# Three stage starts of a five-stage kernel: normalization ahead of the constants, a semaphore clear behind the first gathers, and an interleaved opening of the last stage

## The reference, cut to what matters

```python
x = x + L0_attn(layernorm(x))   # scan mixer: causal conv, state scan, gate, projection
x = x + L0_ffn(layernorm(x))    # h = layernorm(x); 3-tap conv, 16-head causal attention,
                                # then an expert MLP with one of 4 experts per token
x = x + L1_attn(layernorm(x))   # conv, silu, layernorm, decay exp(delta*A), gate, projection
x = x + L1_ffn(layernorm(x))    # 16 experts: sigmoid scores, best 2 of 4 groups, best 4 experts,
                                # out = sum_e cw_e * relu(x W1_e)^2 W2_e + relu(x Ws1)^2 Ws2
```

## Time and profile before

| | us |
|---|---|
| median of 3 runs | 3261.33 |
| lowest and highest of them | 3254.24, 3273.67 |
| the profiled execution, its own time | 3269.45 |
| its span, first to last instruction | 3267.6 |
| TensorE busy | 2776.8 (85%) |
| VectorE busy | 2128.2 (65%) |
| ScalarE busy | 1628.7 (50%) |
| POOL busy | 1028.5 (31%) |

### The profile page before, as it was taken

How to read it: one execution, slowest core, us unless ns; L and a number is a source line. 1 busy time by engine, 2 the same in 40 slices (tenths; PEclk the granted TensorE clock), 3 DMA queues, 4 the chain that set the end, 5 groups by cost and what they waited for, 6 DMA issues and landing times.

```text
span 3267.6 us, 40411 instructions
## 1 busy us (share of the span) xinstructions
PE 2776.8 (85%) x13719; PEld 1674.1 (51%) x13782; DVE 2128.2 (65%) x3827; ACT 1628.7 (50%) x2433; POOL 1028.5 (31%) x715
## 2 busy tenths in 40 slices
PE   7878887887664789999969999878889887999999
PEld 3445454454452455555536666534344444666666
DVE  0689888889794667777522222146777784777776
ACT  2778777877851345555431111157777781111111
POOL 0888888888861212121010000011121000010000
PEclk9899999999777899999979999978999998999999
DMA  3587888888764765555341000100000002000000
GB/s 109 114 171 152 172 174 169 148 177 175 167 145 90 184 180 92 87 86 88 49 151 49 24 25 23 40 25 7 7 10 11 1 1 59 7 10 11 7 7 13
DMA packets 119272, 262.94 MB, mean 80 GB/s; under 512 B 14784, under 2 KB 72896, under 8 KB 117408
## 3 DMA queue, kind: packets, MB, share of 16 engines
q0 software_dynamic: 24928, 134.89, 19.9%
q1 hardware_dynamic: 94144, 125.47, 16.6%
HBM read 135.40 MB, written 131.20 MB: 82 GB/s over the span
## 4 chain that ended last, share of the span: by engine, by line
PE 52%; ACT 6%; DVE 5%; issue 4%; DMA 1%; POOL 0%; SPq 0%; POOLq 0%; ACTq 0%; DVEq 0%
PE PS L1620 7%; PE PS L2331 7%; PE PS L2349 6%; PE PS L1642 4%; PE PS L1911 4%; PE PS L1284 2%; PE PS L1961 2%; ACT Z L2069 2%; PE PS L1919 2%; PE PS L1263 2%; PE PS L1266 2%; PE PS L1211 2%; PE PS L1241 2%; PE PS L1979 1%; PE PS L1943 1%
## 5 line engine op out<-in xcount | busy, mean ns | idle before, releaser
L804 POOL TENSOR_TENSOR Z<-Z 128x1024 f32<-128x1024 f32 x256 | 647.4, 2749 | 52.8 <-DMA Z<-rows_b 52.7
L714 DVE TENSOR_TENSOR_SCAN Z<-PS,Z 128x1024 f32<-128x1024 f32 x256 | 576.3, 2274 | 17.8 <-POOL Z L804 14.5
L508 PE MATMUL PS<-Z 128*128 128x128 f32 x2048 | 301.3, 293 | 122.0 <-DVE Z L714 49.6
L508 PEld LDWEIGHTS PS<-Z 128*128 128x128 f32 x2048 | 246.8, 150 | 254.6 <-issue 79.9
L646 ACT ACTIVATE PS<-Z 128x511 f32<-128x511 f32 x512 | 332.8, 687 | 68.2 <-DVE Z L714 67.7
L1378 ACT ACTIVATE Z<-PS 128x512 f32<-128x512 f32 x320 | 189.0, 596 | 268.7 <-PE PS L1266 258.0
L2382 ACT ACTIVATE Z<-PS 128x512 f32<-128x512 f32 x144 | 85.9, 596 | 416.8 <-PE PS L2331 416.8
L2331 PE MATMUL PS<-Z 128*128 128x512 f32 x576 | 273.7, 600 | 17.6 <-DVE Z L2464 17.6
L658 ACT ACTIVATE Z<-PS,Z 128x512 f32<-128x512 f32 x378 | 245.5, 683 | 70.0 <-PE PS L508 64.2
L1472 DVE TENSOR_REDUCE Z<-PS 128x1 f32<-128x512 f32 (+2 forms) x384 | 182.6, 507 | 121.7 <-PE PS L1242 118.0
L2069 ACT ACTIVATE Z<-Z 128x2048 f32<-128x2048 f32 x128 | 252.4, 1996 | 12.8 <-PE PS L1961 9.9
(11 more groups left out here) (289 smaller groups left out, 5029.8 us busy)
## 6 DMA issues: line engine op xcount, KB each, us to landing
sums<-Z POOLq DMA_DIRECT2D x112, 768.0 KB, 8.7
Z<-rows_b SPq DMA_DIRECT2D x128, 256.0 KB, 4.8
Z<-scr SPq DMA_DIRECT2D x256, 128.0 KB, 5.2
rows_n<-in_L_ffn_expert_wv POOLq DMA_DIRECT2D x32, 528.0 KB, 8.1
scr<-Z SPq DMA_DIRECT2D x32, 384.0 KB
Z<-Z POOLq DMA_DIRECT2D x14, 768.0 KB, 7.6
Z<-in_L_ffn_expert_wv SPq DMA_DIRECT2D x4, 2048.0 KB, 14.9
Z<-sums SPq DMA_DIRECT2D x7, 768.0 KB, 6.3
```

The source lines that it names most:

```text
L508: ins = e.transpose(self.turned[i % 2][:, c * 128:(c + 1) * 128], self.h(k, c // 2)[:, c % 2, i * 128:(i + 1) * 128], ident)
L714: e.tensor_tensor_scan(h, a, h, 0.0, ALU.mult, ALU.add).then_inc(s["scan"], 1)
L804: e.tensor_tensor(self.h(k, f), self.du[b % 2][:, 2 * f:2 * f + 2, :], b3(self.Bs[k % 2], 1, [128, 2, 512]), ALU.mult).then_inc(s["hin"], 1)
```

## The change

In B, VectorE's constants become a step `consts` at n = -45, behind the second normalization and ahead of the transposes and the taps. Inside it, the wait for POOL's pads is gone (ScalarE's copies, which the taps wait for, keep theirs). TensorE's two waits stand in the first `heads`, ScalarE's in the first `weight`. In D, the clear of stage C's semaphores moves from the end of C into D's `fetch`, behind the four gathers of batch 0. In E, TensorE waits for `d_w` at hidden 0 and VectorE at prep 7, the semaphore of the experts' weights becomes four, each for one group of four experts, and the opening of batch 0 follows the list `START`: five preps, hidden 0, preps 5 to 7, hidden 1, preps 8 to 14, the two downs of the shared expert, hidden 2, preps 15 and 16, hidden 3 and 4, prep 17, hidden 5; from then on come the downs of piece 1 and the order as before. The change has no part in stages A and C; stage A's scan mixer already sums in two chains of accumulating DMAs (even and odd states) in the kernel before.

```diff
--- before.py
+++ after.py
@@ -1037,6 +1037,8 @@
         (33, ("valued", 0), ("values", 1)), (34, ("valued", 1)))
 
     EARLY = -26
+
+    CONSTS = -45
 
     def __init__(self, m):
         self.m = m
@@ -1100,6 +1102,8 @@
         out = []
         for n in range(self.PREP[0][0] - 40, 10 * (N + L + 2)):
             q, u = divmod(n, 10)
+            if n == self.CONSTS:
+                out.append(("consts",))
             if n == self.EARLY:
                 out.append(("load", 0))
             if q % 2 and u == 0 and q > 0:
@@ -1186,9 +1190,6 @@
 
     def pe(self, e):
         m, s, ring, ident = self.m, self.s, self.ring, self.m.ident
-        e.wait_ge(s["d_w"], 80)
-        e.wait_ge(s["ready"], 1)
-
         def bank(*step):
             r = self.uses[step]
             if r >= 2:
@@ -1204,6 +1205,9 @@
                 ins.then_inc(s["prod"], 1)
 
         def heads(b, j4):
+            if b == 0 and j4 == 0:
+                e.wait_ge(s["d_w"], 80)
+                e.wait_ge(s["ready"], 1)
             e.wait_ge(s["hc"], b + 2)
             o = bank("heads", b, j4)
             col = ((j4 // 2) + 2 * (j4 % 2)) * 128
@@ -1370,6 +1374,8 @@
 
         def weight(q, u):
             n = 10 * q + u
+            if n == 0:
+                e.wait_ge(s["ready"], 2)
             e.wait_ge(s["st"], n + 1)
             if n >= 8:
 
@@ -1392,20 +1398,19 @@
                 e.wait_ge(*self.made["route", g // 2 - 1, 6])
             e.activation(self.yf[:, g % 2, :], self.end, ACT.Copy).then_inc(s["end"], 1)
 
-        e.wait_ge(s["ready"], 2)
         self.walk(rstd=rstd, rstd2=rstd2, flipped=flipped, high=high, middle=middle, valued=valued, rowed=rowed, weight=weight,
                   pved=pved, featured=featured, route=self.route.act_steps(e))
 
     def dve(self, e):
         m, s, ring, own = self.m, self.s, self.ring, self.m.own["dve"]
-        e.wait_ge(s["d_w"], 80)
-        e.tensor_copy(m.maskb, self.mask).then_inc(s["ready"], 1)
-        e.wait_ge(s["hc"], 1)
-        self.route.dve(e)
-        e.wait_ge(s["d_sel"], 32)
-        for j in range(2):
-            ins = e.tensor_copy(self.sel[:, 4 * j:4 * j + 4, :].rearrange(FLAT), self.pt[j][0:96])
-        ins.then_inc(s["ready"], 1)
+        def consts():
+            e.wait_ge(s["d_w"], 80)
+            e.tensor_copy(m.maskb, self.mask).then_inc(s["ready"], 1)
+            self.route.dve(e)
+            e.wait_ge(s["d_sel"], 32)
+            for j in range(2):
+                ins = e.tensor_copy(self.sel[:, 4 * j:4 * j + 4, :].rearrange(FLAT), self.pt[j][0:96])
+            ins.then_inc(s["ready"], 1)
 
         def stats(b):
             dve_stats(e, own, lambda i: m.X[:, 4 * b + i, :], self.sb).then_inc(s["moments"], 1)
@@ -1500,7 +1505,7 @@
             rr = m.R2[:, 4 * b + 2 * j:4 * b + 2 * j + 2, :].rearrange(FLAT)
             e.tensor_tensor(rr, rr, self.end, ALU.add).then_inc(s["end"], 1)
 
-        self.walk(stats=stats, norm=norm, stats2=stats2, norm2=norm2, taps=taps, turned=turned, swapped=swapped, most=most,
+        self.walk(consts=consts, stats=stats, norm=norm, stats2=stats2, norm2=norm2, taps=taps, turned=turned, swapped=swapped, most=most,
                   rowed=rowed, backed=backed, projected=projected, route=self.route.dve_steps(e))
 
     def pool(self, e):
@@ -2205,6 +2210,8 @@
                 e.indirect_dma_start(self.gy[i % 4], None, self.c.rows_y,
                                      bass.IndirectOffsetOnAxis(ap=self.c.posy[:, i:i + 1], axis=0)).then_inc(
                                          *self.d_gy.over(i))
+            if b == 0:
+                m.clear(e, 3)
 
         def zx(b):
             e.wait_ge(s["gate"], b + 1)
@@ -2222,6 +2229,9 @@
 
 
     PIECES = 18
+
+    START = (range(5), ("hidden", 0, 0), range(5, 8), ("hidden", 0, 1), range(8, 15), ("down", 0, 0, 0), ("down", 0, 0, 1),
+             ("hidden", 0, 2), range(15, 17), ("hidden", 0, 3), ("hidden", 0, 4), range(17, 18), ("hidden", 0, 5))
 
     def __init__(self, m):
         self.m = m
@@ -2248,16 +2258,19 @@
         self.s = {n: m.sem("e_" + n) for n in (
             "d_w", "moments", "rstd", "nt", "prod", "sig", "ms", "gp", "gmax", "rkd", "rkp", "cw", "up", "relu", "hid",
             "dn", "acc")}
-        self.d_e = m.sem("e_d_e")
+        self.d_e = [m.sem(f"e_d_e{g}") for g in range(4)]
         self.steps = self.order()
 
     def order(self):
-        out = [("prep", 0, p) for p in range(self.PIECES)]
+        out = []
+        for what in self.START:
+            out += [("prep", 0, p) for p in what] if isinstance(what, range) else [what]
         for b in range(NB):
             at = 0
-            out += [("hidden", b, 0), ("hidden", b, 1), ("hidden", b, 2), ("down", b, 0, 0), ("down", b, 0, 1)]
+            if b:
+                out += [("hidden", b, 0), ("hidden", b, 1), ("hidden", b, 2), ("down", b, 0, 0), ("down", b, 0, 1)]
             for x in range(16):
-                if x < 15:
+                if x < 15 and (b or x > 2):
                     out.append(("hidden", b, 3 + x))
                 for i in range(2):
                     out.append(("down", b, 1 + x, i))
@@ -2280,9 +2293,9 @@
         e.dma_start(self.ws2, d["Ws2_t"].rearrange("(k p) m -> p k m", p=128)).then_inc(s["d_w"], 16)
         for g in range(4):
             e.dma_start(self.w1[:, 8 * g:8 * g + 8, :], d["W1_t"][4 * g:4 * g + 4].rearrange(
-                "e (k p) m -> p (e k) m", p=128)).then_inc(self.d_e, 16)
+                "e (k p) m -> p (e k) m", p=128)).then_inc(self.d_e[g], 16)
             e.dma_start(self.w2[:, 4 * g:4 * g + 4, :], d["W2_t"][4 * g:4 * g + 4].rearrange(
-                "e p m -> p e m")).then_inc(self.d_e, 16)
+                "e p m -> p e m")).then_inc(self.d_e[g], 16)
         for b in range(NB):
             e.wait_ge(s["acc"], 34 * (b + 1))
             e.dma_start(m.out.rearrange("b (i p) c -> b p i c", p=128)[b],
@@ -2291,7 +2304,6 @@
 
     def pe(self, e):
         m, s, ring, ident = self.m, self.s, self.ring, self.m.ident
-        e.wait_ge(s["d_w"], 64)
 
         def prep(b, p):
             nf = self.nf[b % 2]
@@ -2324,8 +2336,10 @@
                 e.wait_ge(*ring.done(3 * b + 1))
             if n >= 2:
                 e.wait_ge(s["hid"], n - 1)
-            if j == 2 and b == 0:
-                e.wait_ge(self.d_e, 128)
+            if b == 0 and j == 0:
+                e.wait_ge(s["d_w"], 64)
+            if b == 0 and j >= 2 and j % 4 == 2:
+                e.wait_ge(self.d_e[j // 4], 32)
             for k in range(2):
                 w = self.ws1[:, k, 128 * j:128 * j + 128] if j < 2 else self.w1[:, 2 * (j - 2) + k, :]
                 ins = e.matmul(self.up[n % 2], w, self.nf[b % 2][:, k, :], start=k == 0, stop=k == 1)
@@ -2544,7 +2558,7 @@
                 for n, g in enumerate(stages):
                     g.pool(e)
                     m.stage_end(e, n + 1)
-                    if n < 3:
+                    if n < 2:
                         m.clear(e, n + 1)
```

## The result

The kernel after takes 3250.57 us (median of 20 runs, 3239.05 to 3256.39), the kernel before, run beside it on the same chip, 3264.28 (20 runs). The ratio is 0.9958, 95% interval 0.9945 to 0.9970: a gain of 13.7 us, 9.8 to 18.0. Predicted were 27.1 us and 3234.2, in 3224 to 3249; the result lies outside the range, and as a gain of 0.42% it belongs to what the prediction called within 0.5%.

What follows compares the result with a forecast made beforehand. It took one uncovered chain, held by constants or a semaphore clear, to bound the starts of B, D and E; 10.6 + 2.7 + 13.8 = 27.1 us off 3261.3 gave 3234.2, range 3224 to 3249.

Steps and rivals of the forecast that it cites:

- third rival: Starts of B and E: something other than constants releases the chains; 13 to 16 us at most remain, 3248; chance 0.07.
- Stage B, 10.6: Start of B: statistics start with the stage, the taps begin right behind the sel casts, 10.6 us sooner.
- Stage D, 2.7: Start of D: memset and gathers issue 2.7 us sooner and land 2.7 us sooner; range down to 0.
- Stage E, 13.8: Start of E: hidden 6 starts at 37.0 us instead of 50.8, gain 13.8, bounds 12.0 and 16.2.
- (a): Start of E: the statistics no longer wait for constants, saving 5.9 us; TensorE is free for hidden 0 at 6.6.
- (b): TensorE's order in E's start: hidden 0 3.8 us at low clock, logits 1.8 and hidden 1 1.72 at full clock.
- (c): Start of E: VectorE becomes the chain, `cw` is there at 28.4 us and hidden 6 starts at 37.0.
- The bound for low-clock logits: Start of E: logits at the low clock cost 1.8 us more, giving 12.0 as the lower bound of the gain.
- Stops for instructions: Starts of B and E: one or two instruction-loading stops cut the gain to 21.3 or 15.4, 3240 to 3246; chance 0.11.
- Rival 2: Stage E: threading gains nothing because VectorE's queue delays TensorE; only 5.9 remains there, 19.2 in all, 3242; chance 0.11.
- Rival 4: Stage E: the clock stays at its lower level through batch 0, kernel 38 us longer, 3299; chance 0.03.
- three signs: Idle time called issue in a start, hidden 6 after 43 us in E, or low clock past hidden 1.

Runs made afterwards that it cites:

- b_memset: The kernel after with three of POOL's memsets in stage B moved behind the second normalization: 3246.83 us, ratio 0.9949 to the kernel before.
- e_warm: The kernel after with four full-width TensorE products, result unread, added at stage E's start: 3244.91 us, ratio 0.9933 to the kernel before, stage E 544.5.
- e_h1_first: The kernel after with hidden 1 put ahead of the logits in stage E: 3247.82 us, ratio 0.9946 to the kernel before, stage E 550.2.
- d_late: The kernel after with stage D's weight loads issued only once VectorE has added the first gathered tile: 3250.87 us, ratio 0.9967 to the kernel before.

## Why the prediction was wrong, point by point

**What bounds the starts.** Right: each start was one chain, and both waits named were for constants. The third rival, that the change does not do what it says, is out: statistics stand 0.06 to 0.07 us behind the starts of B and E, and B keeps at least 6.1 us to its end.

**Stage B, 10.6.** The mechanism and the order of events were right; 8.8 came at the taps. The step that failed is the 7.7 us from the statistics' start to the normalization's end, carried over from a time when POOL had long filled its pads: in the new place it took 10.0 (to 994.94), and the memsets cost 2.35 of it. b_memset takes them away and meets the predicted 11.3. Over the whole stage, the eight profiles with this change as written have 681.4 to 685.9, the five without 692.0 to 699.5: at least 6.1, and 12.0 by their means (683.3 and 695.3). What goes beyond 8.8 lies in TensorE's stops with nothing to wait for. Those of over 2 us add up to 12.4 to 17.3 us a profile in the five, 15.0 in the mean, and to 10.0 to 14.0 in the eight, 11.9 in the mean. Without them B takes 679.2 to 682.3 in the five and 670.0 to 673.4 in the eight, and the means are 8.8 apart, just what the taps gained. Whether the stops got 3.2 us shorter by the change or by chance, the runs don't show.

**Stage D, 2.7.** The bounds 0 to 2.7 held, the value taken did not: 1.3. The failed step is "that row shows the queues sharing", read from 2124 to 2126, when four fifths of the weights had been moved, and used for gathers issued in the first 4 us. There they got 4.0% beside 62.8%.

**Stage E, 13.8: the step that decided.** The gain was 6.3, below the lower bound of 12.0. (a) held: 5.9 from the waits, 6.3 measured with the old order. (b) failed at "the logits 1.8 at the full clock". The prediction took from 2739.31 that the clock comes back after one hidden piece. That piece stood behind an idle time, and the 5.30 us of the same trace's hidden 0 and 1, at the place that the forecast was for, were not read. In after the clock stood at 1.2 GHz through hidden 0, logits, hidden 1 and four halves of the downs. In (c), what this added reached VectorE through product 1, for which it stood 2.86 us idle, and moved `cw` and hidden 6 by 5.0; hidden 6 and what surrounds it, at the lower clock once more, took the rest. The bound for low-clock logits counted 1.8 us once, where the same cause acted on everything up to 22 us. At the full clock the chain of VectorE was priced rightly: from the end of the logits to `cw` e_warm takes 16.2 us, the forecast's 14.8 + 1.4, and after 19.8. As a difference the sum holds there too: hidden 6 moves from 48.0 to 33.8, 14.2 us, and the stage by 12.9, for 13.8. That `cw` came 2.7 sooner than its 28.4 is because the forecast mixed the clocks, hidden 0 at the lower one and the logits right behind it at the full one; that the difference still comes out so near is in part luck.

**The rivals.** Stops for instructions (0.11): none of TensorE's in the starts is longer than 0.73 us. In B they stand at the same places of the program with every kernel, the first 90 to 92 us behind the stage's start without the change and 83 to 84 with it as written; the one of the earlier trace rows in the chain of waits of after:

```profile
1067.87 4.76 issue
```

The Trainium skill ("Runtime: NRT & Kernel Launch", section "Instruction fetch mechanics") says that crossing a block of instructions is mostly hidden. If these stops are such crossings, which no run here shows, that does not fit the 4.76 us of this row; it fits the starts, which have none of that length.

Rival 2 (0.11), that the threading gains nothing and only the 5.9 remain, is what happened, through the chain it names, TensorE to VectorE and back, but driven by the clock; its time of 3242 was still 8 too low. Rival 4 named the clock and priced it only if it stayed low through batch 0; it was low for 22 us, and low again from 40 on for hidden 6. Of the three signs that were to show the prediction wrong, this one came (the low clock past hidden 1); no long idle time called issue stood in a start, and hidden 6 at 42.0 stayed below the 43. The fault was to hold the clock's price as a case of 0.03 and in full, instead of as a term between.

**The sum.** By stages 8.8 to 12.0, 1.3 and 6.3 make 16.4 to 19.6; the whole kernels give 13.7 and 15.4, with 9.8 to 18.0 for the first. The 16.4 fits both, and the prediction's 27.1 fits neither. A second error is small beside it: the forecast subtracted from the median of three runs, 3261.3, where twenty runs give 3264.3. So of the 16.4 us between 3234.2 and 3250.57, 13.4 are gain that did not come and 3.0 are the base. The first pair of profiles showed 26.2 by B's 10.5, E's 6.5 and D's 10.1, less 1.0 by which A was longer; of the 10.1 the change explains 1.3, and most of the rest is the stretch of lower clock.

## What to carry to other kernels

When a chain is moved into an idle stretch, price TensorE's part of it at the lower clock, unless a row of the same trace shows the same kinds of instructions at the full clock in such a place, and put that into the lower bound for every instruction of the chain. Here four wide products ahead of the chain, in time that is idle anyway, made an interleaving worth 7.8 us of its stage that was worth 0.2 without them. Split such a change into its waits and its order before you believe either. And look what else runs at the time a step moves to: a share of the DMA queues, or a neighbour's memset, has to be read from that time, not from where the step stood.

## What the runs showed of the hardware that was not expected

- The granted clock stayed at 1.2 GHz through 15.4 us with TensorE busy 13.9 (0.50 in both windows of after); the work was four wide instructions, sixteen of 16 columns, four wide ones and the first downs. In e_h1_first, with eight wide ones in a row, the logits right behind them took 1.85 us instead of 3.43, as at 2.4 GHz.
- The mean clock was 0.85 over 40 us in which TensorE had no gap, and 1.00 in the same place of another execution; the stage D around it was 8 to 11 us longer.
- POOL's memsets stretch VectorE's normalization from 1.38 to 3.73 us, and a cast from 0.22 to 1.50.
- A gather with no weights beside it was being added 2.9 us after its issue (d_late); issued among 1.2 MB of weights, gathers took 7.3 to 8.4 (after).
